# Banded attention with a folded matrix per head: scores from one 128x128 product, values with the output projection inside

## The reference

```python
xq = _rms_norm(x @ wq, q_norm_w, EPS)      # wq, wk, wv: [128, 1024]; the norm runs over all 1024 columns
xk = _rms_norm(x @ wk, k_norm_w, EPS)
xv = x @ wv
q, k, v = (t.reshape(B, T, 8, 128).transpose(0, 2, 1, 3) for t in (xq, xk, xv))
rel = pos[None, :] - pos[:, None]
bias = where((rel > 0) | (rel < -16), NEG, slopes * rel)
scores = einsum('bhqd,bhkd->bhqk', q, k) / sqrt(128) + bias
probs = softmax(scores)
y = einsum('bhqk,bhkd->bhqd', probs, v).transpose(0, 2, 1, 3).reshape(B, T, 1024)
return y @ wo                               # wo: [1024, 128]
```

## Time and profile before

| | us |
|---|---|
| median of 3 runs | 1383.39 (1383.28 to 1384.54) |
| the profiled execution | 1387.55 |
| its span in the profile | 1385.7 |
| PE busy in the span | 1263.2 (91%) |
| DVE, ACT, POOL busy | 987.1, 929.9, 507.5 |
| stage D in the trace | about 998 to 1228 |

### The profile page before, as it was taken

One profiled execution on the slowest core, in us unless ns is written; L12 is line 12 of the kernel. 1 busy time (PEld: TensorE's weight loads), 2 busy tenths in 40 slices (PEclk: granted clock), 3 DMA queues, 4 the chain that ended last, 5 costly groups with the idle time before them and its releaser, 6 DMA issues.

```text
span 1385.7 us, 17134 instructions
## 1 busy us (share of the span) xinstructions
PE 1263.2 (91%) x6134; PEld 697.4 (50%) x6134; DVE 987.1 (71%) x1816; ACT 929.9 (67%) x1200; POOL 507.5 (37%) x359
## 2 busy tenths in 40 slices
PE   6999999999999999988888888999899999977666
PEld 3455544444554445423222225777666776853444
DVE  7777777667777677657889882456468767758895
ACT  3999999999999998945677764455455445523321
POOL 2444444444444444754556430233200000025333
PEclk9999999999999999977999997999999999989777
DMA  8200000000000000100000000000100000000000
GB/s 178 61 1 1 0 0 1 0 0 1 1 1 0 0 1 1 62 1 16 1 0 1 2 0 1 0 1 1 57 1 1 1 0 1 1 1 1 0 8 23
DMA packets 27711, 15.01 MB, mean 11 GB/s; under 512 B 16638, under 2 KB 26476, under 8 KB 27500
## 3 DMA queue, kind: packets, MB, share of 16 engines
q1 hardware_dynamic: 27628, 13.92, 3.8%
HBM read 12.86 MB, written 1.05 MB: 10 GB/s over the span
## 4 chain that ended last, share of the span: by engine, by line
PE 78%; DVE 12%; issue 5%; POOL 2%; ACT 2%; DMA 0%; POOLq 0%; SPq 0%; ACTq 0%; DVEq 0%
PE PS L1854 16%; PE PS L1863 8%; DVE ARENA L977 5%; PE PS L850 4%; PE PS L1835 4%; PE PS L1169 4%; PE PS L833 4%; PE PS L754 3%; PE PS L1177 2%; PE PS L705 2%; PE PS L1200 2%; PE PS L721 2%; PE PS L1880 2%; PE PS L1192 2%; PE PS L1823 2%
## 5 line engine op out<-in xcount | busy, mean ns | idle before, releaser
L2216 DVE TENSOR_SCALAR ARENA<-PS,ARENA 128x512 f32<-128x512 f32 x256 | 189.9, 749 | 57.2 <-PE PS L1854 38.6
L1854 PE MATMUL PS<-ARENA 128*128 128x512 f32 x512 | 227.4, 597 | 3.1 <-issue 2.3
L2352 POOL TENSOR_TENSOR ARENA<-ARENA 128x1024 f32<-128x1024 f32 x64 | 151.0, 2360 | 126.6 <-ACT ARENA L2044 122.0
L977 DVE TENSOR_REDUCE ARENA<-PS 128x1 f32<-128x512 f32 x256 | 161.0, 681 | 32.5 <-PE PS L721 32.1
L895 ACT ACTIVATE ARENA<-PS 128x1024 f32<-128x1024 f32 x128 | 128.3, 1025 | 49.7 <-PE PS L740 49.6
L1854 PEld LDWEIGHTS PS<-ARENA 128*128 128x128 f32 x512 | 95.6, 191 | 115.1 <-issue 112.4
L2028 ACT ACTIVATE ARENA<-ARENA 128x2048 f32<-128x2048 f32 x64 | 122.2, 1911 | 33.6 <-DVE ARENA L2216 33.2
L2036 ACT ACTIVATE ARENA<-ARENA,consts_sb 128x2048 f32<-128x2048 f32 x64 | 127.7, 1996 | 0.4
L1863 PE MATMUL PS<-ARENA 128*64 128x512 f32 x512 | 118.4, 605 | 0.9 <-DVE ARENA L2216 0.9
L2044 ACT ACTIVATE ARENA<-ARENA 128x2048 f32<-128x2048 f32 x64 | 118.3, 1896 | 0.0
L2194 DVE TENSOR_SCALAR ARENA<-PS,BT 64x512 f32<-64x512 f32 x64 | 48.0, 749 | 79.2 <-PE PS L1835 75.6
(11 more groups left out here) (258 smaller groups left out, 2595.3 us busy)
## 6 DMA issues: line engine op xcount, KB each, us to landing
ARENA<-in_window_bias_dram SPq DMA_DIRECT2D x1, 1536.0 KB, 6.7
WKVG<-in_L_attn_W_in_dram SPq DMA_DIRECT2D x3, 448.0 KB, 6.9
X<-in_x_dram SPq DMA_DIRECT2D x4, 256.0 KB, 5.0
W<-in_L_ffn_w_dram SPq DMA_DIRECT2D x1, 1024.0 KB
out_dram<-X SPq DMA_DIRECT2D x4, 256.0 KB, 2.2
WQ<-in_L_attn_W_in_dram SPq DMA_DIRECT2D x2, 448.0 KB, 8.4
BV<-in_L_attn_b_in_dram SPq DMA_DIRECT2D x1, 512.0 KB, 6.5
Wout<-in_L_attn_W_out_dram SPq DMA_DIRECT2D x1, 512.0 KB, 4.7
```

Source lines behind the costliest of these rows:

```text
L977: dve.tensor_reduce(NMX[:, w % 2, t, h:h + 1], bank(("cS", n, j)), AX.X, ALU.max, negate=True).then_inc(sem("c_max"), 1)
L1854: done(pe.matmul(o, SK[:, hd, kt * P:(kt + 1) * P], MQ[:, hd, :], start=True, stop=True), ("S", u, c))
L2216: dve.tensor_scalar(D[:, u % 2, hd, kt, :], bank(("S", u, c)), K2[:, u % 2, kt, hd:hd + 1], 1e-30, ALU.add, ALU.max).then_inc(sem("guarded ...
L2352: pool.tensor_tensor(WPAIR, D[:, u % 2, hd, 0:2], D[:, u % 2, hd, 2:4], ALU.add).then_inc(sem("w_paired"), 1)
```

## The change

Two products of weights are formed on chip. For each head h, M_h = wq_h diag(q_norm_w * k_norm_w) wk_h^T and N_h = wv_h wo_h, both 128x128. The RMS factors stay on the two copies of the input, so a head's scores are (M_h^T xq)^T xk with the scaled and turned inputs. The values x N_h already have the form of the output, and the heads' results only need to be summed.

- Router: PE turns wv too (8 more transposes), and forms N (16 matmul records) between the Gram matrices and the turn of the router's weights. DVE multiplies the turned wq by the norms' weights after the router's own arithmetic. In expert step 1 PE forms M (16 records). ACT copies M over wq and N over wv.
- Stage D: one product a head and batch (`dM`) in place of two; DVE evacuates the even heads and ACT the odd ones, as plain copies. Keys for the scores are read from XQK.
- `finish` sums all 8 heads of a tile into the tile's columns of one bank (`dO`), which stays open for a batch's 5 tiles; it is evacuated once a batch by ACT (`sum_out`), turned by 4 transposes (`turn_out`), and added by DVE. YT1, its copies and the 32 products with wo are gone. DVE reads the stream's new value one loop step later than before.
- Banks: stage D rotates over banks 0 to 5, and banks 6 and 7 are for `dO`.

```diff
+    jobs += [(("gn", half), 1, [("folded_values", half + 1)]) for half in range(2)]
...
+        if i == 1:
+            jobs += [(("gm", half), 1, [("folded_scores", half + 1)]) for half in range(2)]
...
+POOLS = {"all": range(BANKS), "D": range(0, 6), "DO": range(6, 8), "A": range(0, 7), "out0": range(7, 8), "cS": range(0, 3), "cV4": range(3, 4), "cP": range(4, 8)}
...
-            for i in range(4):
+            for i in range(6):
                 m, half = divmod(i, 2)
...
-                    mm = pe.transpose(o[:, c * P:(c + 1) * P], WQK1[m][:, k:k + P], ident)
+                    mm = pe.transpose(o[:, c * P:(c + 1) * P], (WQK1 + [WV1])[m][:, k:k + P], ident)
...
+            pe.wait_ge(sem("gram_turned"), 6)
+            for half in range(2):
+                o = begin(("gn", half))
+                for c in range(4):
+                    mm = pe.matmul(o[:, c * P:(c + 1) * P], WVT[:, 4 * half + c, :], WO1[:, 4 * half + c, :],
+                                   start=True, stop=True)
+                done(mm, ("gn", half))
...
+                if i == 1:
+                    pe.wait_ge(sem("folded_weights"), 1)
+                    for half in range(2):
+                        o = begin(("gm", half))
+                        for c in range(4):
+                            mm = pe.matmul(o[:, c * P:(c + 1) * P], WTS[:, 4 * half + c, :], WT[1][:, 4 * half + c, :],
+                                           start=True, stop=True)
+                        done(mm, ("gm", half))
...
+            link(dve.tensor_tensor(W8, BN[:, cq:cq + HD1], BN[:, ck:ck + HD1], ALU.mult))
+            dve.wait_ge(sem("gram_turned"), 2)
+            dve.tensor_tensor(WTS, WT[0], W8.unsqueeze(2).to_broadcast([P, HD1, P]), ALU.mult
+                              ).then_inc(sem("folded_weights"), 1)
...
                     for h in range(HD1):
-                        for m, key in enumerate(("dQ", "dK")):
-                            o = begin((key, b, h))
-                            done(pe.matmul(o, WQK1[m][:, h * P:(h + 1) * P], XQK[:, b % 2, m], start=True, stop=True),
-                                 (key, b, h))
+                        o = begin(("dM", b, h))
+                        done(pe.matmul(o, MQK1[:, h * P:(h + 1) * P], XQK[:, b % 2, 0], start=True, stop=True),
+                             ("dM", b, h))
...
-                    mm = pe.matmul(o[0:nq, h, :], QT1[:, h, q0:q0 + nq], KT1[:, h, k0:k0 + P], start=True, stop=True)
+                    mm = pe.matmul(o[0:nq, h, :], QT1[:, h, q0:q0 + nq], XQK[:, b % 2, 1, k0:k0 + P],
+                                   start=True, stop=True)
...
-                o = begin(("dY", n)).rearrange("p k (h c) -> p (k h) c", c=P)
+                o = begin(("dO", b)) if ti == 0 else bank(("dO", b))
                 for h in range(HD1):
-                    mm = pe.matmul(o[:, h, 0:nq], V1[:, n % 4, h * P:(h + 1) * P], PT1[:, n % 2, h, 0:nq],
-                                   start=True, stop=True)
-                done(mm, ("dY", n))
+                    mm = pe.matmul(o[:, q0:q0 + nq], V1[:, n % 4, h * P:(h + 1) * P], PT1[:, n % 2, h, 0:nq],
+                                   start=ti == 0 and h == 0, stop=ti == len(TILES1) - 1 and h == HD1 - 1)
...
-                    pe.wait_ge(sem("d_y"), n + 1)
-                    o = begin(("out1", b))
-                    for t in range(QT):
-                        for h in range(HD1):
-                            mm = pe.matmul(o[:, t * P:(t + 1) * P], YT1[:, h, t * P:(t + 1) * P], WO1[:, h, :],
-                                           start=h == 0, stop=h == HD1 - 1)
-                    done(mm, ("out1", b))
...
+            def turn_out(b):
+                pe.wait_ge(sem("d_ot"), b + 1)
+                o = begin(("out1", b))
+                for t in range(QT):
+                    mm = pe.transpose(o[:, t * P:(t + 1) * P], OT1[:, t * P:(t + 1) * P], ident)
+                done(mm, ("out1", b))
...
-                    for h in range(HD1):
-                        full(act, ("dK", b, h))
-                        c = NCOL["L1_attn_k_norm_w"] + h
-                        act.activation(KT1[:, h], bank(("dK", b, h)), ACT.Copy, scale=BN[:, c:c + 1]).then_inc(sem("d_k"), 1)
+                    for h in range(1, HD1, 2):
+                        full(act, ("dM", b, h))
+                        act.copy(QT1[:, h], bank(("dM", b, h))).then_inc(sem("d_k"), 1)
...
+            def sum_out(b):
+                full(act, ("dO", b))
+                if b:
+                    full(act, ("out1", b - 1))
+                act.copy(OT1, bank(("dO", b))).then_inc(sem("d_ot"), 1)
...
-                dve.tensor_copy(YT1[:, :, q0:q0 + nq], bank(("dY", n)).rearrange("p k (h c) -> p (k h) c", c=P)[:, :, 0:nq]
-                                ).then_inc(sem("d_y"), 1)
-                if ti == len(TILES1) - 1:
-                    add_to_stream(3, b, ("out1", b))
...
                 if stats_next(n) is not None:
+                    add_to_stream(3, stats_next(n), ("out1", stats_next(n)))
                     stats(4, stats_next(n))
-            finish(STEPS1 - 1)
+            add_to_stream(3, B - 1, ("out1", B - 1))
```

More of the change, by code:

```diff
@@ L309, in stage_c_jobs, with norm_jobs, turned_out_batch @@
         if b and e == 5:
-            jobs += norm_jobs(b - 1)
+            jobs += norm_jobs(b - 1, "all")
     jobs += [(("fW", i), 1, [("f_w", i + 1)]) for i in range(3)]
     return jobs
-def norm_jobs(b):
-    return [(("z", b, m), 1, [("zy", 2 * b + m + 1)]) for m in range(2)]
+def norm_jobs(b, pool):
+    return [(("z", b, m), 1, [("zy", 2 * b + m + 1)], pool) for m in range(2)]
+def turned_out_batch(n):
+    b, ti = divmod(n - 1, len(TILES1))
+    return b - 1 if ti == 0 and 1 <= b < B else None
 def stage_d_jobs():
-    jobs = [(("yt", 0, m), 1, [("xqk", m + 1)]) for m in range(2)]
+    jobs = [(("yt", 0, m), 1, [("xqk", m + 1)], "D") for m in range(2)]
     steps = B * len(TILES1)
@@ L342, in stage_d_jobs @@
             jobs += start(n + 2)
+        if turned_out_batch(n) is not None:
+            jobs += turn_out(turned_out_batch(n))
         if n:
             jobs += finish(n - 1)
[L345 to L348, removed]
+        if n >= 9 and (n - 4) % len(TILES1) == 0:
+            jobs += ln_job(4, n // len(TILES1) - 1, "D")
+        jobs += [(("dT", n), 2, [("d_pt", n + 1)], "D")]
+    return jobs + finish(steps - 1) + turn_out(B - 1)
 def stage_e_jobs():
@@ L911, in scalar_c @@
             act.activation(ROUTER["exp"], ROUTER["shifted"], ACT.Exp).then_inc(sem("r_exp"), 1)
-            for i in range(4):
+            for i in range(6):
                 m, half = divmod(i, 2)
                 full(act, ("gt", i))
-                act.copy(WT[m][:, 4 * half:4 * half + 4, :].rearrange("p c d -> p (c d)"), bank(("gt", i))
+                act.copy((WT + [WVT])[m][:, 4 * half:4 * half + 4, :].rearrange("p c d -> p (c d)"), bank(("gt", i))
                          ).then_inc(sem("gram_turned"), 1)
@@ L919, in scalar_c @@
                 act.copy(GM[:, m, :], bank(("gg", m))[:, 0:P]).then_inc(sem("gram"), 1)
+            for half in range(2):
+                full(act, ("gn", half))
+                act.copy(NVO1[:, 512 * half:512 * half + 512], bank(("gn", half))).then_inc(sem("folded_values"), 1)
             for b in range(B):
@@ L929, in scalar_c @@
                                    ).then_inc(sem("h1_ready"), 1)
+                if i == 1:
+                    for half in range(2):
+                        full(act, ("gm", half))
+                        act.copy(MQK1[:, 512 * half:512 * half + 512], bank(("gm", half))).then_inc(sem("folded_scores"), 1)
                 if early(i, 1) is not None:
@@ L1211, in tensor_d @@
                     start(n + 2)
+                if turned_out_batch(n) is not None:
+                    turn_out(turned_out_batch(n))
                 if n:
@@ L1293, in vector_d, with summed @@
             stats(3, B - 1)
+            def summed(n):
+                b, ti = divmod(n, len(TILES1))
+                if ti == len(TILES1) - 1:
+                    full(dve, ("dO", b))
+                else:
+                    dve.wait_ge(sem("d_summed"), n - b + 1)
             def scale_y(b):
@@ L1306, in start @@
                         scale_y(b + 1)
-                    for h in range(HD1):
-                        full(dve, ("dQ", b, h))
-                        c = NCOL["L1_attn_q_norm_w"] + h
-                        dve.tensor_scalar(QT1[:, h], bank(("dQ", b, h)), BN[:, c:c + 1], None, ALU.mult).then_inc(sem("d_q"), 1)
+                    for h in range(0, HD1, 2):
+                        full(dve, ("dM", b, h))
+                        dve.tensor_copy(QT1[:, h], bank(("dM", b, h))).then_inc(sem("d_q"), 1)
                 nq, kind = TILES1[ti][1], TILES1[ti][3]
```

53 lines of the change are left out of this document (30 added, 23 removed).

## The result

| | before | after |
|---|---|---|
| median us | 1383.34 (1382.85 to 1384.54, 4 runs) | 1328.68 (1327.68 to 1330.90, 4 runs) |
| the profiled execution, its span | 1387.55, 1385.7 | 1330.9, 1329.1 |

The ratio is 0.9606, 95% interval 0.9582 to 0.9630: 54.7 us less. The forecast was 1332.5, its own range 1328 to 1340, near whose lower end the result lies. The span is 56.6 us shorter.

What follows compares the result with a forecast made beforehand. PE was taken as the limit, with DVE and ACT waiting for it in stage D. Terms -59.2 + 3.5 + 1.8 + 3.0 = -50.9 us took the profiled 1387.55 to 1336.6; the median, 4.2 lower, was forecast at 1332.5, range 1328 to 1340.

Steps and rivals of the forecast that it cites:

- (1) to (3): Stage D: half the Q and K products, the wo product, and the last batch's uncovered end are saved; -59.2 us.
- (4): Router: 8 more transposes and 16 records of N on PE add 3.5 us, bounds 2.7 to 3.9.
- (5): Expert step 1: forming M, 16 records on PE, adds 1.8 us, between 0 and 3.
- (6): Stage E's start: PE's clock falls without the long product before it, slowing query products; +3.0 us, between 0 and 5.
- The bias table's transfer: Stage D's beginning: the 1.5 MB transfer has 7 us less before first use, but lands in time; at nothing.
- the nine waits for banks: Stage D: six turns and three values products wait for banks; put at nothing, up to 11 us if the layout is off.
- A: Rival, stage D: DVE takes over as limit; 1348 if 16 inner steps cost 1 us more each; chance 0.14.
- B: Rival: the clock falls within stage D, half its PE work at half clock adding 82 us, 1415; chance 0.03.
- C: Rival, stage D: summing 8 heads into one open bank makes products wait for each other; 35 us, 1368; chance 0.03.
- (1): Stage D: half of the Q and K products go, 16 records or 6.88 us a batch, 27.5 us over four batches.

Runs made afterwards that it cites:

- kernel after once more: The changed kernel measured a second time with nothing changed, in a second set of 6 runs; 1331.86 us, ratio 0.9626 to the kernel before.
- values alone: The kernel after with queries and keys as before, so only the value and output matrices are folded; 1358.12 us, ratio 0.9801 to the kernel before.
- scores alone: The kernel before with only the query and key matrices folded, values and output products as they were; 1355.81 us, ratio 0.9795 to the kernel before.
- the last kernel: The kernel with unread products at three places, plus three more in PE's waits ahead of the router's products; 1324.97 us, ratio 0.9578 to the kernel before.

## Why the prediction came out

**The limit.** The argument was that PE sets stage D since the chain's pieces abut and both other engines wait. It held: periods of 38.81 and 39.24 for "about 39", and work added to PE is paid whole. One detail of the reading was too smooth: before, the chain did not abut on PE all through a batch, but passed over DVE for some 4 us ahead of each L1200 (1073.62 to 1077.71). PE worked beside that and stood idle for 0.7, which the prediction had in its sum.

The weight loads are busy 29.68 of 39.00 us in the batch that PE fills, 76%. The Trainium skill (Trainium Kernel Development and Optimization, Best Practices) says to judge the distance to the roofline by the share of the peak arithmetic and by the weight loads' busy share, not by matmul busy time. The prediction read this as a measure of what a removal returns, by which a quarter of the gain would have been missing. Nothing was missing, and PE work added to these batches was paid whole. That says nothing against the rule as a measure of roofline distance; it does not tell which engine sets the time of this stage.

**(1) to (3), removals, -59.2 forecast, -59.03 measured** from the stage's start to the addition. That the sum is right to 0.2 us is partly luck, since within it two errors of 1 us and more cancel. The first batch gave 5.46 for 6.88: its products fell from 15.79 to 9.90 only, as 16 records at the low clock lose 3.0 against full clock where 32 lost 2.0, and DVE stands on the chain until 1028 while the pipeline fills. The fourth gave 24.28 for about 23.3. In the kernel after once more the first batch gave 6.2 and the sum is 59.8. From the last values to the addition it is 1.4 us, expected under 2.

**(4) the router, +3.5 forecast with bounds 2.7 to 3.9, +1.56 measured.** This is the term that was mis-sized, below its lower bound. The chain of the kernel after:

```profile
856.32 4.03 PE PS L831 x24
860.35 3.57 PE PS L837 x32
863.92 1.79 PE PS L843 x16
865.71 1.75 PE PS L850 x16
```

N, L843, costs the 1.79 that the low estimate had. The eight added transposes should have cost 0.9 to 1.8, but turns and Gram records together take 7.60 where they took 7.64 with eight fewer. The clock has a part in it; kernel before, then after:

```profile
856.00:860.00 4.00, 4.00 (x20) 4.00 (x20) 0.04 (x1) 0.00 (x0) 0.00 (x0) 0.50 0.00 0
860.00:864.00 4.00, 4.00 (x20) 4.00 (x20) 3.28 (x12) 2.49 (x5) 0.00 (x0) 0.50 0.01 4
```

```profile
856.00:860.00 4.00, 4.00 (x25) 4.00 (x26) 2.96 (x11) 2.36 (x6) 0.00 (x0) 0.63 0.00 0
860.00:864.00 4.00, 4.00 (x39) 4.00 (x38) 3.56 (x14) 1.38 (x5) 0.00 (x0) 1.00 0.00 0
```

Before, half clock (1.2 GHz) lasts to 864; after, it ends some 5 us sooner, while the turns begin only 3.6 us sooner. So the two traces are not alike at this place, and +1.56 mixes the change with it. Traces in which the router's products took the same time are alike. The kernel with one more product a step has them at 6.63, as before:

```profile
851.50 6.63 PE PS L822 x32
858.13 4.96 PE PS L831 x24
863.09 3.57 PE PS L837 x32
```

From the turns on it takes 12.06 us, as values alone does, against 9.58 before: the change costs 2.5. Where the products took 3.47 to 3.49, it is 11.44 (four kernels) against 9.56 (scores alone, whose router has only the 16 old transposes and no N): 1.9, since PE stood waiting 0.64 of the 9.56 for DVE's router arithmetic, which the new work covers. The eight transposes cost 1.45 where the products took 6.63, but they also push the Gram records and those behind them further into the full clock: 3.57 for 4.13. This is what the prediction lacked: its bounds held the clock of this stretch fixed and varied only the record's price. At full clock throughout, in the last kernel, the four pieces take 9.78.

**(5) M in the expert steps: +1.78**, forecast 1.8. **(6) stage E's start: +2.46**, forecast 3.0 (+1.8 in the kernel after once more): query products 4.65 for 3.44, value products 2.07 for 1.16 and transposes 0.85 for 0.52. The clock fell, as forecast, but rose again within the query products, 0.58 a record where 0.86 or 0.43 was expected; half of the cost lies in the pieces ahead of them. That the size fits is therefore partly luck. The mechanism is shown by the kernels with unread products.

**What was put at nothing.** The bias table's transfer (window 998 to 1002, 375 GB/s) holds nobody up: no engine's wait in stage D is put down to it. From 1010 to 1156 PE waits once for DVE's copy of values, 0.4 us, once 0.7 at the fourth batch's start, and in the first batch at most 0.7 at a time. So the nine waits for banks, up to 11 us if the layout was off, cost 0.4 at most.

**The rivals.** A (1348) needs DVE to be late in inner steps; DVE has 1.4 us of slack there, and it takes two passes a step to get the form of trace that A describes. B: the clock is 1.00 in the inner batches. C: 16 records summed into one open bank take 1.77 as 16 apart did. The Trainium skill (TensorE: Matmul & The Clock Gate, Back-to-back issue gap) gives 216 ns for 512 columns by its formula for a single product, without a word on the type; an estimate by it would have made (1) 13.8 us. The 16 float32 records gone took 6.88 a batch, 430 ns each, and the measurement decides.

**The median.** -50.9 was forecast; -54.7 was measured, and -53.1 in the second set. Of the 3.8, about 2 is (4) as the traces have it (1.0 to 1.6 like for like), 0.5 is (6), and the rest is of the size by which the two sets of runs of the kernel after differ (1328.68 and 1331.86). How near the forecast came within these 3 us is luck; that stage D's terms hold batch by batch is not.

## What to carry to other kernels

Where the chain's pieces abut on one engine in each step, what is taken from that engine comes back at its full length and separate savings add up; price it from that chain, record by record. Before relying on it, lay out the strictest step of the next engine: here 1.4 us of slack in a step of 6.25 let 14.6 us a batch through, and two more passes of 1.2 us made that engine the limit. Look at what a removed long product did for TensorE's clock, and at where the clock stands in short serial stretches such as a router: that was the largest error of the sum.

## What the hardware showed beside that

The same instructions of the router's products (32 records of 8 columns) took 3.47 to 3.49 us in six of the twelve traces, 5.33 to 5.43 in three and 6.63 in three, by the clock at that moment; it differs between executions of the same kernel (5.40 and 3.47). This does not by itself explain the 3 to 6 us by which runs of a kernel spread: in the two traces of the kernel after the expert steps begin at 867.46 with products of 5.40, and at 870.17 with products of 3.47. Where the rest comes from is open.

Products that nobody reads, 0.43 us a record, put into waits of PE, held the granted clock at 1.00 at the start of stage D in every trace that had them, and at the start of stage E in two of three. There they delayed nothing; in the third the clock dipped among them and they stood about 0.9 us in the way.
